# Placing the shared expert's output products and the state sums on TensorE in a selective-scan and MoE kernel

## The chip, the cores and the metric

The kernel runs on one core of a Trainium2 chip. Its metric is the device time of one execution in microseconds (us). Three runs of the kernel before gave 1494.33, 1497.56 and 1495.76 us, median 1495.76.

## The reference

The program is two layers of "cross-attention replaced by a selective scan" and a feed-forward part, on x of shape (4, 512, 512) and a context of shape (4, 512, 256):

```python
x = x + tanh(g_xattn[0]) * scan_layer(ctx_1024, layernorm(x), L0...)   # z = layernorm(x)
x = x + tanh(g_ffn[0])   * moe(layernorm(x), L0...)
x = x + tanh(g_xattn[1]) * scan_layer(ctx_1024, layernorm(x), L1...)
x = x + tanh(g_ffn[1])   * lora_ffn(layernorm(x), L1...)

# scan_layer, for one of 4 batches; 512 channels, 16 states, 512 steps
x = in_proj_w @ hidden; u = silu(conv4(x) + conv_b)
dt_lo, Bm, Cm = split(x_proj_w @ u); delta = softplus(dt_proj_w @ dt_lo + dt_proj_b)
state_t = state_{t-1} * exp(delta_t * A) + delta_t * u_t * B_t        # every channel and state
y_t = sum_n state_t[n] * C_t[n] + D * u_t;   y = y * silu(z)

# moe, per token, 16 experts, the best 4 by grouped routing
y_e = (silu(x @ gate_e.T) * (x @ up_e.T)) @ down_e.T
out = sum_e w_e * y_e + shared expert (the same form, for all tokens)
```

Everything is float32.

## The kernel before

Work is cut by batch and layer into eight stages: stages 0 to 3 are the scans of layer 0, stage 4 is the first scan of layer 1 (`FIRST_B` is 5, `NB` is 4), stages 5 to 7 are the other scans of layer 1 and run beside the tiles of the routed experts; a tail follows. Each engine runs a program of its own, written out by hand; they meet only at semaphores. An engine executes its program in order, so an instruction that waits holds up all that is written behind it.

A stage's scan is 32 units, four turns `i` of eight units `c`. I write a unit as (stage, turn, unit), for instance (4, 1, 3), and leave the stage out where it is plain. One unit covers one state and half of the 512 channels (256 channels as two rows of 128 partitions by 512 steps). It passes through four engines:

- ScalarE computes the decay exp(delta * A) (`decay`, line 712).
- VectorE multiplies du by B into PSUM (`mul_b`, line 1704), then does the scan (line 1712) into one of four slots `W[c % 4]`.
- GpSimd multiplies the slot by C (`mul_c`, line 457). It waits until the `mul_b` of the next unit is done.
- TensorE adds the slot to banks 0 and 1 by two products with the identity (`sum_state`, line 1095) and frees the slot. The scan four units later waits for that.

Between these units stand the other parts. Those that the change touches belong to the shared expert of the batch two stages back (`g`) or one stage back (`f`):

- `shared_in(b, it)`, line 1144: 16 rows of the trace (8 products) into the two auxiliary banks `AUX`; ScalarE's tanh (line 755) and VectorE's `shared_hidden` (lines 1736 and 1738) make the hidden half from them.
- `shared_out(b, (0, 1))` and `shared_out(b, (2, 3))`, line 1152: four products each, for two of the four row tiles, into `AUX[0]` and `AUX[1]`. VectorE's `shared_add` (line 1744) adds each bank to x. The second pair waits for `shacc`, that is, until VectorE has read the first.
- VectorE calls `shared_add(g, (0, 1))` after unit (s, 0, 7) and `shared_add(g, (2, 3))` after unit (s, 1, 2). These places are the same in both kernels.

After turn 1 of stage 4 comes the turn to the experts. VectorE ranks the last batch's tokens (`route`, from line 1536 on), does `shared_hidden(f, 0)`, and works out the slots (`slots`, from line 1598 on, with `shared_hidden(f, 1)` behind it). TensorE meanwhile has `shared_in`, two counting products (lines 1285 and 1286) which wait for `ranked` and for the first hidden half, `x_proj`, the second `shared_in`, and `stay_warm(PRE[1], 56)`, 56 products of 128 by 128 whose result nobody reads (line 1046). Turn 2 of stage 4 then mixes the units with eight `index_round`s (line 1172), each of which waits for masks from ScalarE (`mark_rows`) and VectorE (`mark_chunks`). Mask n uses a ring of three buffers: from n = 3 on it waits for index round n - 3.

Of the kernel before, what the change touches and what calls it, by code (L numbers as in the profile page):

```python
# [26 lines left out]
NB, L, D = 4, 512, 512  # L27
DM, NS, DR, DC = 256, 16, 16, 4
ET, QT, KC = D // P, L // P, DM // P
# [40 lines left out]
def build(nc, t):  # L70
    with ExitStack() as ctx:
# [80 lines left out]
        PRE = [PS[:, 4], PS[:, 5]]  # L152
# [853 lines left out]
        def _(pe):  # L1006
# [36 lines left out]
            def stay_warm(bank, n):  # L1043

                for _ in range(n):
                    nc.tensor.matmul(bank[:, 0:P], ID[:, :], ON[:, :], start=True, stop=True)  # L1046
# [100 lines left out]
            def shared_out(b, qs):  # L1147
                pe.wait_ge(shh_ready, IT * (b + 1))
                for q in qs:
                    for it in range(IT):  # L1150
                        at = 2 * WGU + it * D
                        mm = nc.tensor.matmul(AUX[q % 2], HB[:, it, q * P:(q + 1) * P], MW[:, 0, at:at + D],  # L1152
                                              start=(it == 0), stop=(it == IT - 1))
                    mm.then_inc(shdown_done, 1)
# [54 lines left out]
            for s in range(FIRST_B):  # L1209
                f, p, g = s - 1, s + 1, s - 2  # L1210
                if f >= 0:
                    conv(p, 0)
                    conv(p, 1)
                if f >= 0:
                    pe.wait_ge(yg_done, f + 1)
                sum_skip(s, 0)
                for c in range(HPT):
                    sum_state(s, 0, c)
                    if f < 0 and c == 0:
                        conv(p, 0)  # L1220
                        conv(p, 1)
                    if c == 0 and f >= 0:
                        if g >= 0:

                            pe.wait_ge(shh_ready, IT * (g + 1))
                        y_transposes(f, Y[:, yslot(f)], (0, 1))
                    if c == 1 and f >= 0:
                        in_proj(p, 1)
                        y_transposes(f, Y[:, yslot(f)], (2, 3))
                    if c == 3 and g >= 0:  # L1230
                        pe.wait_ge(xacc, QT * (f + 1))
                        shared_out(g, (0, 1))
                    if c == (6 if s == NB else 7) and g >= 0:

                        pe.wait_ge(shacc, QT * g + 2)
                        shared_out(g, (2, 3))
                    if c == 3 and f < 0:
                        in_proj(p, 1)
                    if f >= 0 and c in (4, 5):
                        conv(p, c - 2)  # L1240
                    if f < 0 and c == 5:
                        conv(p, 2)
                        conv(p, 3)
                if s == NB:
                    break
                for i in range(1, TURNS - 1):
                    for c in range(HPT):
                        sum_state(s, i, c)
                        if i == 1 and c == 1:
                            x_proj(p)  # L1250
                        if i == 1 and c in (4, 7):
                            dt_proj(p, c // 7)
                for c in range(HPT):
                    sum_state(s, TURNS - 1, c)
                    if c == 0 and f >= 0:
                        if g >= 0:
                            pe.wait_ge(shacc, QT * (g + 1))
                        norm_transposes(f, XN, range(ET))
                    if c == 1 and f >= 0:
                        route(f)  # L1260
                    if c == 2 and f >= 0:
                        shared_in(f, 0)
                    if c == 4:
                        in_proj(p + 1, 0)
                    if c == 5 and f >= 0:
                        shared_in(f, 1)

            s, f, p = NB, NB - 1, NB + 1
            for c in range(HPT):
                sum_state(s, 1, c)  # L1270
                if c == 1:
                    pe.wait_ge(shacc, QT * f)
                    norm_transposes(f, XN, (0, 1))
                if c == 2:
                    norm_transposes(f, XN, (2, 3))
                if c == 3:
                    route(f)
                if c == 5:

                    shared_in(f, 0)  # L1280

            pe.wait_ge(ranked, NB)
            pe.wait_ge(shh_ready, IT * f + 1)
            sel = SEL[:, :, :].rearrange("p t e -> p (t e)")
# [2 lines left out]
            x_proj(p)  # L1287
            pe.wait_ge(counts_read, 1)
            shared_in(f, 1)
            pe.wait_ge(u_ready, ET * (p + 1))  # L1290
            stay_warm(PRE[1], 56)
            shared_out(f, (0, 1))
            for c in range(HPT):
                if c == 0:
                    pe.wait_ge(shacc, QT * f + 2)
                    shared_out(f, (2, 3))
                else:
                    index_round(c - 1)
                sum_state(s, 2, c)
                if c in (3, 5):  # L1300
                    dt_proj(p, c // 5)
            for c in range(HPT):
# [790 lines left out]
```

## Time and profile before

| | |
|---|---|
| median of three runs | 1495.76 us |
| the profiled execution's own time | 1494.33 us |
| its span in the profile | 1492.6 us |
| TensorE busy | 1281.0 us (86%) |
| VectorE busy | 1352.1 us (91%) |
| ScalarE busy | 970.8 us (65%) |
| GpSimd busy | 785.6 us (53%) |
| granted TensorE clock, mean | 0.949 of full speed |

Times in the rows count from the span's start. PE is TensorE, DVE is VectorE, ACT is ScalarE, POOL is GpSimd. A float32 product of TensorE stands in the trace as two records, so x8 in a timeline row is four products. The ends of pipelined products are modelled: how long one group took is read better from the start of the next group. In a timeline row the last bracket is how long the engine stood idle before it, and who ended that.

### The profile page before, as it was taken

What the parts mean: (1) busy time and instruction counts of PE and PEld (TensorE: products, weight loads), DVE (VectorE), ACT (ScalarE), POOL (GpSimd) and SP (SyncE); (2) the same over time, 40 slices, a digit from 0 to 9 for tenths busy, and PEclk for the clock granted to TensorE, in tenths of its full rate; (3) what the DMA queues carried; (4) which work ended last, traced back from release to release, by engine and by line L of the source; (5) the groups of instructions that cost most, each with busy time, mean ns of one, the idle gap of its engine ahead of it and who ended that gap; (6) DMA issues with size and microseconds to landing.
All of it is one profiled execution on the core that took longest, in us unless ns stands there. A gap on an engine that the chain in (4) does not pass through costs nothing.

```text
span 1492.6 us, 14767 instructions
## 1 busy us (share of the span) xinstructions
PE 1281.0 (86%) x4630; PEld 740.3 (50%) x4630; DVE 1352.1 (91%) x1319; ACT 970.8 (65%) x1528; POOL 785.6 (53%) x411
## 2 busy tenths in 40 slices
PE   7785796899689869999989998899988899927988
PEld 3331242443244324455556676666766666616555
DVE  4999999899999999998998989999899989888894
ACT  5866568475866665635956788777887767734442
POOL 0465566545545553450565555665565665566632
PEclk9898899799999998999999999999999999977999
DMA  8354445535554553460466788787787887855531
GB/s 259 100 149 126 127 143 141 155 85 154 139 143 101 143 130 111 107 169 22 109 186 228 240 271 282 236 263 244 257 275 234 282 277 272 274 178 152 168 97 57
DMA packets 99838, 264.32 MB, mean 177 GB/s; under 512 B 10832, under 2 KB 11344, under 8 KB 93616
## 3 DMA queue, kind: packets, MB, share of 16 engines
q1 hardware_dynamic: 87936, 225.36, 50.5%
q0 software_dynamic: 11440, 37.50, 7.7%
q8 instruction: 37, 0.61, 0.2%
q10 hardware_dynamic: 384, 0.52, 0.1%
q14 instruction: 41, 0.34, 0.1%
HBM read 233.73 MB, written 29.62 MB: 176 GB/s over the span
## 4 chain that ended last, share of the span: by engine, by line
PE 41%; DVE 26%; issue 7%; ACT 6%; DMA 5%; POOL 4%; DVEq 0%; SPq 0%; ACTq 0%; POOLq 0%
DVE state L1712 11%; PE banks L1185 11%; DVE banks L1704 8%; PE banks L1196 6%; PE banks L1095 6%; DMA expert_w<-in_moe_w 3%; PE banks L1144 2%; PE banks L1164 2%; PE banks L1355 2%; PE banks L1039 2%; PE banks L1152 2%; ACT decay L712 2%; ACT L712 1%; POOL state L457 1%; PE banks L1016 1%
## 5 line engine op out<-in xcount | busy, mean ns | idle before, releaser
L457 POOL TENSOR_TENSOR state<-state,bc_rows 128x1024 f32<-128x1024 f32 x254 | 599.2, 2360 | 605.9 <-DVE banks L1704 605.7
L1712 DVE TENSOR_TENSOR_SCAN state<-decay,banks 128x1024 f32<-128x1024 f32 x176 | 401.9, 2284 | 15.7 <-ACT decay L712 6.6
L1095 PE MATMUL banks<-state,ident 128*128 128x512 f32 x640 | 330.0, 650 | 94.0 <-POOL state L457 93.8
L1704 DVE TENSOR_TENSOR banks<-du,bc_rows 128x1024 f32<-128x1024 f32 x256 | 314.5, 1228 | 13.4 <-DVE state L1712 0.5
L1185 PE MATMUL banks<-z_gate,expert_w 128*128 128x256 f32 (+1 forms) x1504 | 284.5, 347 | 6.4 <-DMA expert_w<-in_moe_w 6.4
L1185 PEld LDWEIGHTS banks<-z_gate,expert_w 128*128 128x128 f32 x1504 | 249.3, 191 | 59.4 <-issue 21.4
L1095 PEld LDWEIGHTS banks<-state,ident 128*128 128x128 f32 x640 | 121.3, 202 | 269.6 <-POOL state L457 153.6
L712 ACT ACTIVATE decay<-delta,neg_a 128x511 f32<-128x511 f32 x352 | 226.4, 710 | 16.4 <-DVE state L1712 11.2
L1712 DVE TENSOR_TENSOR_SCAN state<-expert_w,banks 128x1024 f32<-128x1024 f32 x80 | 182.9, 2286 | 7.7 <-ACT expert_w L712 5.1
L1196 PE MATMUL banks<-expert_w,hidden 128*128 128x512 f32 x316 | 156.0, 609 | 2.3 <-ACT expert_out L776 1.2
L1723 DVE TENSOR_TENSOR y_scan<-y_scan,state 128x1024 f32<-128x1024 f32 x94 | 114.3, 1216 | 3.6 <-POOL state L457 2.0
L712 ACT ACTIVATE expert_w<-delta,neg_a 128x511 f32<-128x511 f32 x160 | 104.1, 711 | 8.5 <-DVE state L1712 7.7
L762 ACT ACTIVATE z_gate<-banks 128x512 f32<-128x512 f32 (+1 forms) x94 | 49.6, 529 | 74.8 <-PE banks L1164 74.1
L712 ACT ACT_TABLE_LOAD x65 | 83.4, 1283 | 1.6 <-ACT x_dbl L578 0.4
L1046 PE MATMUL banks<-ones,ident 128*128 128x128 f32 x386 | 49.9, 290 | 28.9 <-DVE neg_mean_rstd L1935 28.9
L769 ACT ACTIVATE hidden<-banks 128x256 f32<-128x256 f32 (+1 forms) x94 | 33.2, 353 | 61.1 <-PE banks L1185 60.5
L1196 PEld LDWEIGHTS banks<-expert_w,hidden 128*128 128x128 f32 x316 | 54.4, 197 | 34.5 <-issue 30.9
L1046 PEld LDWEIGHTS banks<-ones,ident 128*128 128x128 f32 x386 | 49.0, 205 | 38.2 <-issue 38.2
L1144 PE MATMUL banks<-y_scan,expert_w 128*128 128x512 f32 x128 | 60.9, 632 | 3.4 <-DVE hidden L1738 3.4
L1730 DVE TENSOR_TENSOR hidden<-hidden,banks 128x256 f32<-128x256 f32 (+1 forms) x94 | 35.1, 373 | 31.3 <-ACT hidden L769 30.5
L769 ACT ACT_TABLE_LOAD x47 | 60.3, 1283 | 0.8
L1016 PE MATMUL banks<-ctx_t,in_w 128*128 128x512 f32 x96 | 47.8, 646 | 9.6 <-DMA ctx_t<-in_ctxT 7.2
(318 smaller groups left out, 1679.9 us busy)
## 6 DMA issues: line engine op xcount, KB each, us to landing
bc_rows<-bc_d SPq DMA_DIRECT2D x208, 512.0 KB, 4.9
expert_w<-in_moe_w SPq DMA_DIRECT2D x48, 1536.0 KB, 9.1
ys_d<-expert_out SPq DMA_DIRECT2D x32, 512.0 KB, 5.6
ctx_t<-in_ctxT SPq DMA_DIRECT2D x8, 512.0 KB, 6.7
x_res<-in_x SPq DMA_DIRECT2D x4, 1024.0 KB, 10.7
xn_d<-y_scan SPq DMA_DIRECT2D x4, 1024.0 KB, 7.5
ys_d<-expert_out SPq DMA_DIRECT2D x15, 256.0 KB, 5.7
out_x<-x_res SPq DMA_DIRECT2D x3, 1024.0 KB, 5.9
```

The costliest lines, as they stand in the source:

```text
L457: nc.gpsimd.tensor_tensor(W[:, c % 4], W[:, c % 4], bcast2(BC[:, u, 1, :]), ALU.mult).then_inc(mulc_done, 1)
L712: ins = nc.scalar.activation(DAS[c % n][:, m, 1:], DEL[:, s % 2, et, 1:], ACT.Exp, scale=AN[:, lay(s), et, state:state + 1])
L769: nc.scalar.activation(HT[:, j % 2, it, 0:n], GU(j, it)[:, 0:n], ACT.Silu).then_inc(sil_ready, 1)
L1016: mm = nc.tensor.matmul(pre_bank(s, et), INW[:, k, et * P:(et + 1) * P], CTX[:, k, :], start=(k == 0), stop=(k == KC - 1))
L1046: nc.tensor.matmul(bank[:, 0:P], ID[:, :], ON[:, :], start=True, stop=True)
L1095: mm = nc.tensor.matmul(PS[:, m], ID[:, :], W[:, c % 4, m, :], start=False, stop=True, skip_group_check=True)
L1144: mm = nc.tensor.matmul(AUX[g], MW[:, 0, at:at + P], XNT[:, k, :], start=(k == 0), stop=(k == ET - 1))
L1185: mm = nc.tensor.matmul(GU(j, it)[:, g * TILE:g * TILE + n], MW[:, u % 2, at:at + P], XST[:, k, 0:n], start=(k == 0), stop=(k == ET - 1))
L1196: mm = nc.tensor.matmul(out_bank(j, r), HT[:, u % 2, it, r * P:(r + 1) * P], MW[:, u % 2, at:at + D], start=(it == 0), stop=(it == IT - 1))
L1704: nc.vector.tensor_tensor(drive(s), DU[:, s % 2, 2 * h:2 * h + 2, :], bcast2(BC[:, u, 0, :]), ALU.mult).then_inc(mulb_done, 1)
L1712: nc.vector.tensor_tensor_scan(flat(W[:, c % 4]), flat(DAS[c % da_slots(s, i)]), flat(drive(s)), 0.0, ALU.mult, ALU.add).then_inc(scan_don ...
L1723: nc.vector.tensor_tensor(y, y, W[:, k % 4], ALU.add).then_inc(w_free, 1)
```

## The change

Only TensorE's program changes. The products `shared_out(g, (2, 3))` of stages 2, 3 and 4 are issued later: by one state sum in stages 2 and 3, by two in stage 4. They now stand behind the first sum of turn 1 in all three. In stage 4, `shared_in(f, 0)` goes from between the sums of units 5 and 6 to behind that of unit 7; the 56 warming products and a wait for `u_ready` ahead of them are gone; and in turn 2 the state sum of a unit is issued ahead of, not behind, the `shared_out` or `index_round` of the same step.

```diff
-                    if c == (6 if s == NB else 7) and g >= 0:
-
-                        pe.wait_ge(shacc, QT * g + 2)
-                        shared_out(g, (2, 3))
...
                     for c in range(HPT):
                         sum_state(s, i, c)
+                        if i == 1 and c == 0 and g >= 0:
+                            pe.wait_ge(shacc, QT * g + 2)
+                            shared_out(g, (2, 3))
...
             s, f, p = NB, NB - 1, NB + 1
             for c in range(HPT):
                 sum_state(s, 1, c)
+                if c == 0:
+                    pe.wait_ge(shacc, QT * (f - 1) + 2)
+                    shared_out(f - 1, (2, 3))
...
-                if c == 5:
-
-                    shared_in(f, 0)
-
+
+            shared_in(f, 0)
             pe.wait_ge(ranked, NB)
...
             shared_in(f, 1)
-            pe.wait_ge(u_ready, ET * (p + 1))
-            stay_warm(PRE[1], 56)
             shared_out(f, (0, 1))
             for c in range(HPT):
+                sum_state(s, 2, c)
                 if c == 0:
                     pe.wait_ge(shacc, QT * f + 2)
                     shared_out(f, (2, 3))
                 else:
                     index_round(c - 1)
-                sum_state(s, 2, c)
```

Below, TensorE's instructions stand in a row, before (-) and after (+). One x is one product here. First the end of turn 0 and the start of turn 1 in stage 2; stage 3 reads the same. Line 1095 is the state sum, two products a unit; 1152 is `shared_out`, 1058 `x_proj`.

```order
 L1039 MATMUL banks<-delta,expert_w 128x511
-L1095 MATMUL banks<-state,ident 128x512 x4
-L1152 MATMUL banks<-expert_w,hidden 128x512 x4
-L1095 MATMUL banks<-state,ident 128x512 x4
+L1095 MATMUL banks<-state,ident 128x512 x6
+L1152 MATMUL banks<-expert_w,hidden 128x512 x4
+L1095 MATMUL banks<-state,ident 128x512 x2
 L1058 MATMUL banks<-du,xproj_w 48x512 x4
```

`shared_out(g, (2, 3))` moved one unit's sum back; `x_proj` keeps its place. In stage 4 the same products move two sums back:

```order
-L1095 MATMUL banks<-state,ident 128x512 x2
-L1152 MATMUL banks<-expert_w,hidden 128x512 x4
-L1095 MATMUL banks<-state,ident 128x512 x6
+L1095 MATMUL banks<-state,ident 128x512 x6
+L1152 MATMUL banks<-expert_w,hidden 128x512 x4
+L1095 MATMUL banks<-state,ident 128x512 x2
 L1114 MATMUL banks<-ident,y_scan 128x128 x8
```

Line 1114, the transposes of the normed rows, keeps its place. Last, from the end of turn 1 to the first steps of turn 2 in stage 4: 1131 is TensorE's part of the routing, 1144 `shared_in`, 1046 the warming products, 1088 the start of the second half's sum, 1172 an index round.

```order
 L1131 MATMUL banks<-router_w,y_scan 128x16 x16
-L1095 MATMUL banks<-state,ident 128x512 x4
-L1144 MATMUL banks<-y_scan,expert_w 128x512 x8
-L1095 MATMUL banks<-state,ident 128x512 x4
+L1095 MATMUL banks<-state,ident 128x512 x8
+L1144 MATMUL banks<-y_scan,expert_w 128x512 x8
...
-L1046 MATMUL banks<-ones,ident 128x128 x56
-L1152 MATMUL banks<-expert_w,hidden 128x512 x8
-L1088 MATMUL banks<-y_scan,ident 128x512 x2
+L1152 MATMUL banks<-expert_w,hidden 128x512 x4
```

The first `shared_in` moved behind two more sums, and the second `shared_in` is followed at once by `shared_out`. The instructions of the other engines keep their order.

## Rows read from the trace of the kernel before

**Rows 1.** The page: the chain that ended last, by engine.

```profile
PE 41%; DVE 26%; issue 7%; ACT 6%; DMA 5%; POOL 4%; DVEq 0%; SPq 0%; ACTq 0%; POOLq 0%
```

**Rows 2.** Windows: bounds, length, busy us of PE, PEld, DVE, ACT, POOL; clock, DMA.

```profile
359.00:404.00 45.00, 33.71 (x73) 11.81 (x72) 43.11 (x26) 35.86 (x68) 28.24 (x12) 1.00 0.53 133
```

**Rows 3.** Timeline of PE, stage 2, units (0,6) to (1,1): start, us, group.

```profile
350.70 3.60 PE L1095 MATMUL banks<-state,ident 128*128 128x512 f32 x8
354.13 3.60 PE L1152 MATMUL banks<-expert_w,hidden 128*128 128x512 f32 x8
357.57 3.60 PE L1095 MATMUL banks<-state,ident 128*128 128x512 f32 x8
```

**Rows 4.** Timeline of DVE, the two adds of `shared_add(0, (2, 3))`.

```profile
356.44 0.72 DVE L1744 SCALAR_TENSOR_TENSOR x_res<-banks,tanh_gates,x_res 128x512 f32<-128x512 f32 x1
357.77 0.75 DVE L1744 SCALAR_TENSOR_TENSOR x_res<-banks,tanh_gates,x_res 128x512 f32<-128x512 f32 x1 [0.61 <-PE banks L1152]
```

**Rows 5.** Line 1744: what its idle time ended on, us and times, whole run.

```profile
  PE banks L1152: 3.0, 4
```

**Rows 6.** Timeline of POOL, the product of unit (2, 1, 0).

```profile
349.54 2.35 POOL L457 TENSOR_TENSOR state<-state,bc_rows 128x1024 f32<-128x1024 f32 x1 [1.34 <-DVE banks L1704]
```

**Rows 7.** Timeline of PE, stage 4: `shared_out(2, (2, 3))` and the sums behind it.

```profile
643.69 3.60 PE L1152 MATMUL banks<-expert_w,hidden 128*128 128x512 f32 x8
647.12 5.31 PE L1095 MATMUL banks<-state,ident 128*128 128x512 f32 x12
```

**Rows 8.** Timeline of DVE, stage 4: the same batch's adds, and scan (4, 1, 4).

```profile
646.67 1.40 DVE L1744 SCALAR_TENSOR_TENSOR x_res<-banks,tanh_gates,x_res 128x512 f32<-128x512 f32 x2
655.30 2.29 DVE L1712 TENSOR_TENSOR_SCAN state<-decay,banks 128x1024 f32<-128x1024 f32 x1 [2.40 <-ACT decay L712]
```

**Rows 9.** Timeline of PE, stage 4, from sum (1, 4) to the counting products.

```profile
661.70 6.34 PE L1095 MATMUL banks<-state,ident 128*128 128x512 f32 x8
667.87 7.03 PE L1144 MATMUL banks<-y_scan,expert_w 128*128 128x512 f32 x16
...
679.55 0.67 PE L1285 MATMUL banks<-selected,upper 128*128 128x256 f32 x2 [1.22 <-DVE hidden L1738]
```

**Rows 10.** Timelines of POOL, ACT and DVE in that stretch.

```profile
666.47 4.65 POOL L457 TENSOR_TENSOR state<-state,bc_rows 128x1024 f32<-128x1024 f32 x2 [1.35 <-DVE banks L1704]
...
674.94 0.60 ACT L755 ACTIVATE hidden<-banks 128x512 f32<-128x512 f32 x1 [12.82 <-PE banks L1144]
...
678.01 0.68 DVE L1736 SCALAR_TENSOR_TENSOR hidden<-hidden,banks 128x512 f32<-128x512 f32 x1
```

**Rows 11.** Timeline of PE, stage 4: the warming products and `shared_out(3, (0, 1))`.

```profile
691.12 12.67 PE L1046 MATMUL banks<-ones,ident 128*128 128x128 f32 x112
703.63 3.60 PE L1152 MATMUL banks<-expert_w,hidden 128*128 128x512 f32 x8
```

**Rows 12.** Timeline of DVE: end of `shared_hidden(3, 1)`, adds of (0, 1).

```profile
699.90 0.69 DVE L1738 TENSOR_TENSOR hidden<-hidden,banks 128x512 f32<-128x512 f32 x1
...
705.55 0.75 DVE L1744 SCALAR_TENSOR_TENSOR x_res<-banks,tanh_gates,x_res 128x512 f32<-128x512 f32 x1 [0.79 <-PE banks L1152]
707.26 0.75 DVE L1744 SCALAR_TENSOR_TENSOR x_res<-banks,tanh_gates,x_res 128x512 f32<-128x512 f32 x1 [0.97 <-PE banks L1152]
```

**Rows 13.** Timeline of PE in stage 3: a `shared_in` behind an idle stretch.

```profile
593.09 9.89 PE L1144 MATMUL banks<-y_scan,expert_w 128*128 128x512 f32 x16 [3.36 <-DVE hidden L1738]
```

**Rows 14.** Windows around that `shared_in`; columns as before.

```profile
592.00:596.00 4.00, 2.92 (x4) 1.40 (x5) 3.93 (x4) 3.97 (x6) 1.77 (x1) 0.50 0.01 2
596.00:600.00 4.00, 4.00 (x7) 1.70 (x7) 3.96 (x4) 4.00 (x7) 0.58 (x1) 0.66 0.57 101
```

**Rows 15.** Turns 2 and 3: ACT's mask 3 and decay (3, 4), DVE's scan (3, 4).

```profile
717.86 2.43 ACT L730 ACTIVATE y_scan<-expert_w 128x128 f32<-128x128 f32 x8
...
752.02 2.54 ACT L712 ACTIVATE decay<-delta,neg_a 128x511 f32<-128x511 f32 x4
...
755.65 2.29 DVE L1712 TENSOR_TENSOR_SCAN state<-decay,banks 128x1024 f32<-128x1024 f32 x1
```

## The prediction

> **What bounds the kernel now.** I read the chain of waits first. TensorE holds 41% of it and VectorE 26% [rows 1]; no engine bounds the whole kernel, so a move on TensorE is judged by what waits at its place. The windows say who leads in the scan stages: in the 45 us behind turn 0 of stage 2 VectorE is busy 43.11 us and TensorE 33.71 [rows 2]. There a late TensorE costs nothing and a late VectorE costs all. At the start of a stage it is the reverse: TensorE runs without a gap from the sums (0, 6) on [rows 3], and VectorE waits for it. The idle time of the `shared_add` line shows where: four waits for `shared_out`, 3.0 us in all [rows 5]. One is 0.61 us at the last add of stage 2 [rows 4]; stage 3 repeats it; the other two, 0.79 and 0.97 us, stand in stage 4 behind the warming products [rows 12]. Last I followed stage 4 by timelines of each engine. The change therefore matters at the places where VectorE waits for line 1152 or 1144.
>
> **Stages 2 and 3: `shared_out` behind one more sum.** Eight records of 512 columns take 3.43 us (350.70 to 354.13), so one unit's sum, four records, takes 1.72. TensorE has no gap here, and the sum that is pulled ahead, (1, 0), is ready: its GpSimd product ends at 349.54 + 2.35 = 351.9, before TensorE reaches it at 355.8 [rows 3, 6]. So `shared_out` ends 1.72 us later, at 359.3 instead of 357.6. VectorE was already waiting for that end: its last add starts at 357.77. It now starts at about 359.45, 1.68 later. `x_proj` behind it starts when it did. What the change frees sooner are slots of the scan ring, and no scan of this stretch waited for a slot. VectorE's program goes on without a gap, so nothing gives the 1.68 back: **2 x 1.68 = +3.4 us**. Bounds: 0 if something later absorbs both, 3.4 if nothing.
>
> **Stage 4, first half.** `shared_out(2, (2, 3))` started at 643.69 and ended at 647.12; the three sums behind it fill 5.2 us (5.31 with the modelled end), so they were ready or nearly so [rows 7]. With two of them ahead it ends at 650.56. VectorE comes to its adds at 646.67 [rows 8], does the first when TensorE's half is done (648.9) and the second at 650.65, ending near 651.35 instead of 647.99. That is 3.3 us late. But two units later VectorE had waited 2.40 us for a decay (655.30) [rows 8], and ScalarE's decay waits for TensorE's transposes, whose place and time stay (652.3). So the wait takes up 2.3 of the 3.3: **+1.0 us**, bounds 0 and 3.3.
>
> **The turn to the experts.** `shared_in(3, 0)` started at 667.87 behind the sums of units 4 and 5 [rows 9]. ScalarE made the tanh of it at 674.94, and VectorE picked it up only at 678.01, after its routing [rows 10]: 2.5 us of slack. Now the sums of units 6 and 7 stand ahead. GpSimd ends the product of unit 7 at 666.47 + 4.65 = 671.1, with the delay above 672.1; the sum takes 1.72, `shared_in` 6.87 (twice 3.43), tanh and handover 0.8: 681.5. By the other path, TensorE reaches the sums up to 3 us later than before, since the transposes and its routing products follow state products which wait for the delayed VectorE; then two slow sums (6.2 us, as in rows 9), two fast ones 3.4 and the same tail give about 682.3. VectorE's routing ends at 678.01 + 1.0 = 679.0 and now waits 2.5 to 3.3 us. Behind that wait stand `slots` and everything after it, and the counting products wait for VectorE as before (679.55) [rows 9]. **+3.0 us**, bounds 2.0 and 10 (the latter if `shared_in` runs at the low clock throughout, 6.9 more).
>
> **The warming products.** They hold TensorE from 691.12 to 703.8, while the hidden half that `shared_out(3, (0, 1))` needs is there at 700.6 [rows 11, 12]. So `shared_out` could start 3.2 us earlier. VectorE, however, has unit (4, 2, 0) and a mask to do first, until 704.76, and waited for TensorE only 0.79 + 0.97 = 1.76 us. This is all that can be won. Against it: without them TensorE is idle about 9.5 us ahead of `shared_out` (from the end of `shared_in`, 691.1 by the old times, to 700.6). In stage 3, after 3.36 us idle, a `shared_in` took 9.89 us against 7.03 for the same products elsewhere [rows 9, 13], and the granted clock was 0.50, then 0.66 [rows 14], that is the low level (1.2 GHz) for about five and a half microseconds of work: 2.9 us lost. With the same loss `shared_out` takes 3.43 + 2.9 = 6.3 us and ends at 706.9 (old times) against 707.1. So the gain is **-0.2 us**; bounds -1.8 (clock stays up) and +0.4 (all four products slow, 6.87).
>
> The Trainium skill, "TensorE: Matmul & The Clock Gate", section "HAM oscillation — how this bites in real kernels", puts the loss at half the throttled time and counts a whole burst behind a long idle stretch as throttled. The row of stage 3 agrees for the loss (about 5.6 us at the low level, 2.9 lost) but shows the clock up again within the burst. By the page the term here would be +0.4, by the row -0.2. Its table "Why this matters for your kernels" speaks against taking warming work away ahead of a burst.
>
> **Turn 2.** The sum ahead of the index round makes each round later by up to a state product and a sum. VectorE has no idle time here but the two waits named. ScalarE is nearly full: mask 3 (old start 717.86) [rows 15] waits for index round 0, which now follows sum (2, 1) and ends near 724. Taking VectorE's shift of about 4 us at that point off, ScalarE loses a further 2.2 us. Decay (3, 4), the first of the pair at 752.02, ends 1.3 later, at 753.3, and its scan starts at 755.65 [rows 15]: 2.3 us of slack. VectorE's own masks 3 to 7 wait for index rounds with 0.6 us to spare by the same replay, once short by 0.2. **+0.3 us**, bounds 0 and 3.
>
> **The sum.** 3.4 + 1.0 + 3.0 - 0.2 + 0.3 = +7.5 us. After stage 4 the kernel follows what VectorE and GpSimd hand over at the end of stage 4, by waits on their work, so the shift passes to the end. The profiled execution took 1494.33 us (1492.6 of span and 1.7 around it): 1501.8. It was the lowest of the three, 1.4 us under their median; I put the forecast of a median 0.7 above: **1502.5 us**, +0.45%. What a measurement of this kernel tells from no change is about 0.2%, 3 us, so the line to slower is 1498.8.
>
> **Rivals.**
> *Clock stays up and the moves are hidden* (faster). Place: `shared_out(3, (0, 1))`. If `shared_in` just before keeps the clock high over the idle stretch, VectorE's 1.76 us go. It decides only if the four delays above come to nothing, for instance because TensorE's queue at the stage starts is shorter than the rows say. Against it: the 0.61 us wait is direct evidence that VectorE is tied to that very end. 1494.33 - 1.8 = 1492.5, with the median's offset 1493. Chance 6%.
> *The stage starts absorb.* If the 1.68 us are taken up in the following stage (VectorE waits for decays at the next stage's start too), or the turn to the experts loses only 2.0, the sum is +4 or less: 1495 to 1499. Against it: those decays wait for TensorE, which is itself set off by VectorE's last units. Chance 14%.
> *`shared_in(3, 0)` slow.* With the sums of units 4 to 7 spread out by their waits, the clock may be low throughout; the granted clock after the routing products was already low for two sums (6.34 us for what takes 3.43). +6.9: 1509. Chance 8%.
> *Turn 2 stays slow.* If TensorE never got back to the high clock there, a sum and an index round take 6.9 us a unit against VectorE's 4.3: 8 x 2.6 = +21: 1523. Against it: stage 3's clock recovered under a load that is no denser. Chance 4%.
> *The forecast*, each delay as worked out: 68%.
>
> The range: 1498 to 1508 holds the forecast with its bounds and parts of the second and third rival. Slower: 68 + 8 + 4 + 3 (of the second rival) = 83%. Same: 11%. Faster: 6%.
>
> **What the changed profile would show.** (1) Idle time of line 1744 ended by line 1152: stages 2 and 3 with about 1.3 us before the first add and 1.0 before the second, and in stage 4 two waits, 2.2 and 1.0; with 1.4 us at the third `shared_out` in all near 9 us instead of 3.0. (2) A wait of VectorE of 2.5 to 3.3 us for ScalarE's tanh (line 755) ahead of line 1736 in stage 4, where there is none now. (3) TensorE idle near 9.5 us ahead of the third `shared_out`, its clock near 0.5 there, the group about 6.3 us long. (4) An idle time of ScalarE of about 2 us before mask 3, ended by an index round. (5) The start of the first expert tile's products 7 to 8 us later, and the rest of the span as long as before. The prediction is wrong if (1) shows no longer waits, or if the later stages end up with another length by more than 2 us.

## The result, and the profile after

| | changed kernel | kernel before |
|---|---|---|
| median, us (6 runs each) | 1507.30 (1505.57 to 1513.75) | 1495.99 (1494.33 to 1497.56) |
| ratio, 95% interval | 1.0089 (1.0067 to 1.0110) | |
| profiled execution, us | 1501.42 | 1494.33 |
| its span, us | 1499.7 | 1492.6 |

The change makes the kernel slower by 11.3 us of median, 0.9%. The forecast was +7.5 us on the profiled execution and 1502.5 us for the median. The profiled execution came out at +7.1, but it was quicker than all other runs of the same kernel. Three further times of that kernel are on record (1505.49, 1511.18 and 1512.48 us); the mean of all nine is 1509.25, and it is this that the ratio reflects: 0.89%, or 13.3 us (10.0 to 16.5). The direction was right and 1507.3 lies in the forecast's range (1498 to 1508), but the forecast change of the median, +6.7 us, is 40% below the 11.3 of the medians and half of what the ratio says. Two further rounds of the changed kernel gave 1.0074 and 1.0069. Each ratio below is against the kernel before as timed beside that run; medians of different rounds are not compared.

The engines' shares (the page's first part; busy us, share of the span, instructions) hardly moved:

```profile
PE 1261.5 (84%) x4518; PEld 721.7 (48%) x4518; DVE 1353.0 (90%) x1319; ACT 971.4 (65%) x1528; POOL 784.2 (52%) x411
```

The changed file's VectorE lines stand two lower: `shared_add` is 1742 (it was 1744), `shared_hidden` 1734 and 1736, the masks 1694, the scan 1710. Here is the idle time of line 1742 over the whole run, against 3.0 us in 4 waits before [rows 5]:

```profile
  PE banks L1152: 10.7, 9
```

The waits of VectorE in stage 4, 640 to 762 us (us in total, times, longest); the same stretch before had 2.4 us for a decay and 1.8 for line 1152, 4.2 in all:

```profile
DVE x_res L1742 <- PE banks L1152: 6.3, 5, 2.3
DVE expert_out L1694 <- PE banks L1172: 2.6, 1, 2.6
DVE hidden L1734 <- ACT hidden L755: 2.6, 1, 2.6
```

That is 11.5 us, 7.3 more than before. The entry of line 755 and most of the first were forecast; the one of line 1694, and 1.5 us of the first, were not. Timeline of VectorE, in order of time (start, us, group, idle time before it and what ended it): first stage 2's two adds, which answer to [rows 4]; then stage 4's, which answer to [rows 8], and the scan (4, 1, 4), which waits for no decay now; then the tanh that VectorE had not waited for in [rows 10]; then the third and fourth pair of adds; last a mask of turn 2.

```profile
354.71 0.75 DVE L1742 SCALAR_TENSOR_TENSOR x_res<-banks,tanh_gates,x_res 128x512 f32<-128x512 f32 x1 [1.25 <-PE banks L1152]
356.42 0.75 DVE L1742 SCALAR_TENSOR_TENSOR x_res<-banks,tanh_gates,x_res 128x512 f32<-128x512 f32 x1 [0.96 <-PE banks L1152]
...
646.80 0.75 DVE L1742 SCALAR_TENSOR_TENSOR x_res<-banks,tanh_gates,x_res 128x512 f32<-128x512 f32 x1 [2.30 <-PE banks L1152]
648.51 0.75 DVE L1742 SCALAR_TENSOR_TENSOR x_res<-banks,tanh_gates,x_res 128x512 f32<-128x512 f32 x1 [0.97 <-PE banks L1152]
...
654.13 2.29 DVE L1710 TENSOR_TENSOR_SCAN state<-decay,banks 128x1024 f32<-128x1024 f32 x1
...
679.51 0.69 DVE L1734 SCALAR_TENSOR_TENSOR hidden<-hidden,banks 128x512 f32<-128x512 f32 x1 [2.61 <-ACT hidden L755]
...
708.46 0.75 DVE L1742 SCALAR_TENSOR_TENSOR x_res<-banks,tanh_gates,x_res 128x512 f32<-128x512 f32 x1 [1.53 <-PE banks L1152]
...
718.33 0.75 DVE L1742 SCALAR_TENSOR_TENSOR x_res<-banks,tanh_gates,x_res 128x512 f32<-128x512 f32 x1 [0.51 <-PE banks L1152]
720.04 0.75 DVE L1742 SCALAR_TENSOR_TENSOR x_res<-banks,tanh_gates,x_res 128x512 f32<-128x512 f32 x1 [0.97 <-PE banks L1152]
...
739.83 0.82 DVE L1694 TENSOR_TENSOR expert_out<-expert_w,small 128x632 f32<-128x632 f32 x1 [2.62 <-PE banks L1172]
```

The last three rows are new. The kernel before did the fourth pair of adds in one go at 716.55, and its masks of turn 2 without a wait. The timeline of TensorE says why. The first row answers to the `shared_in` of [rows 9], the second to `shared_out(3, (0, 1))` of [rows 11]; then follow the sum (2, 0) with `shared_out(3, (2, 3))` behind it, and the sum (2, 4) with an index round behind it.

```profile
671.82 7.03 PE L1144 MATMUL banks<-y_scan,expert_w 128*128 128x512 f32 x16
...
702.15 6.27 PE L1152 MATMUL banks<-expert_w,hidden 128*128 128x512 f32 x8 [9.35 <-DVE hidden L1736]
...
712.89 2.54 PE L1095 MATMUL banks<-state,ident 128*128 128x512 f32 x4 [2.75 <-POOL state L457]
715.22 4.79 PE L1152 MATMUL banks<-expert_w,hidden 128*128 128x512 f32 x8
719.84 1.88 PE L1095 MATMUL banks<-state,ident 128*128 128x512 f32 x4
...
734.38 3.53 PE L1095 MATMUL banks<-state,ident 128*128 128x512 f32 x4
737.70 2.09 PE L1172 MATMUL banks<-expert_out,y_scan 128*128 128x79 f32 x16
```

The sum (2, 0) at 712.89 had waited 2.75 us for GpSimd's product, and it and the `shared_out` behind it ran in part at the low level of TensorE's clock: from 712.89 to 719.84 they took 6.95 us, where one and a half groups of 3.43 are 5.15. VectorE's adds came late by 0.51 and 0.97. The sum at 734.38 took 3.53 us where a sum takes 1.9, again at the low level. The index round waited behind it and ended at 739.8, and VectorE's mask starts there. The windows of the three stretches (bounds, length, busy us of PE, PEld, DVE, ACT, POOL, granted clock, DMA) show the level, 0.50 being 1.2 GHz and 1.00 being 2.4; a value between is a mean over both levels:

```profile
700.00:704.00 4.00, 1.85 (x2) 0.84 (x3) 3.79 (x6) 3.33 (x10) 0.00 (x0) 0.50 0.00 0
704.00:708.00 4.00, 4.00 (x7) 1.69 (x6) 2.93 (x3) 3.04 (x7) 0.00 (x0) 0.58 0.01 2
...
712.00:716.00 4.00, 3.11 (x5) 1.35 (x6) 3.97 (x4) 3.29 (x10) 2.04 (x2) 0.77 0.29 93
716.00:720.00 4.00, 4.00 (x9) 1.78 (x8) 2.57 (x3) 3.12 (x6) 1.15 (x1) 0.80 0.36 118
...
728.00:732.00 4.00, 3.40 (x19) 2.29 (x19) 3.97 (x4) 3.97 (x12) 2.04 (x2) 1.00 0.42 132
732.00:736.00 4.00, 4.00 (x12) 1.68 (x12) 3.97 (x4) 4.00 (x11) 2.04 (x2) 0.83 0.37 119
736.00:740.00 4.00, 4.00 (x20) 2.83 (x19) 1.38 (x2) 3.97 (x7) 1.39 (x1) 0.74 0.35 117
```

### Where the 11 us are

VectorE leads in the scan stages, so the distance between two of its scan starts is the time of a stretch. In us, from the scan rows of each trace; (s, i, c) is stage, turn, unit. A to D are the stretches that the change touches: A is (2, 1, 0) to (2, 1, 4), the same as (3, 1, 0) to (3, 1, 4) to 0.01; B is (4, 1, 0) to (4, 1, 4); C is (4, 1, 4) to (4, 2, 0); D1 is (4, 2, 0) to (4, 2, 4); D2 is (4, 2, 4) to (4, 3, 0). M is (2, 1, 4) to (3, 1, 0). "All" is (2, 0, 0) to (5, 0, 0), "rest" what lies outside.

| kernel | A | M | B | C | D1 | D2 | all | rest |
|---|---|---|---|---|---|---|---|---|
| before | 17.64 | 123.59 | 18.21 | 46.46 | 21.68 | 17.26 | 472.23 | 1020.37 |
| before_again | 17.63 | 123.56 | 18.21 | 46.48 | 21.66 | 17.29 | 472.23 | 1025.87 |
| changed | 19.36 | 120.97 | 19.29 | 49.14 | 23.01 | 19.86 | 480.74 | 1018.96 |
| after_again | 19.34 | 123.57 | 19.28 | 50.83 | 22.39 | 19.82 | 484.34 | 1022.36 |
| after_third | 19.35 | 120.98 | 19.28 | 49.16 | 23.02 | 19.86 | 480.74 | 1022.16 |
| after_old_order | 19.35 | 121.00 | 19.28 | 49.16 | 21.34 | 17.27 | 476.54 | 1019.76 |
| after_with_warming | 19.36 | 124.34 | 19.28 | 50.78 | 23.29 | 18.17 | 484.30 | 1022.40 |
| move_2_3_only | 19.36 | 124.50 | 18.21 | 46.45 | 23.33 | 17.26 | 478.19 | 1024.81 |
| shared_out_4_only | 17.63 | 123.62 | 19.28 | 46.45 | 22.38 | 17.28 | 474.03 | 1023.57 |
| shared_in_only | 17.64 | 123.55 | 18.20 | 49.17 | 21.67 | 17.27 | 474.91 | 1025.79 |
| no_warming | 17.63 | 123.56 | 18.21 | 46.46 | 20.85 | 17.27 | 471.39 | 1023.61 |
| order_only | 17.64 | 125.06 | 18.21 | 46.47 | 23.31 | 19.82 | 477.89 | 1028.71 |
| earlier_42 | 16.93 | 124.12 | 16.50 | 46.52 | 20.16 | 17.27 | 468.19 | 1027.81 |
| earlier_56 | 16.93 | 125.20 | 16.49 | 46.48 | 21.88 | 17.26 | 470.93 | 1021.37 |

Changed against before: A +1.72, twice; B +1.08; C +2.68; D +1.33 and +2.60; together 11.1 us, close to the 11.3 of the medians and within the ratio's 10.0 to 16.5. The profiled pair showed 7.1 because M came out 2.6 shorter and the rest 1.4 shorter. M takes either 121.0 or 123.6 and more in kernels with the very same code there. The traces show why: the sum (2, 3, 2) of stage 2, which follows TensorE's routing products, ran at the low level in the kernel before (granted clock 0.57 from 428 to 432 us), and at full clock in the changed one (1.00 from 424 to 432):

```profile
428.49 3.42 PE L1095 MATMUL banks<-state,ident 128*128 128x512 f32 x4
...
425.98 1.96 PE L1095 MATMUL banks<-state,ident 128*128 128x512 f32 x4
```

From its start to the next group it took 3.26 us in the first and 1.80 in the second, and VectorE's waits behind it are 0.95, 0.82 and 2.08 us against 0, 0 and 1.14. `after_again`, the same program as the changed kernel, has it slow (3.35 us) and the longer M. The rest differs by up to 5.5 us between two executions of the kernel before (1020.37 and 1025.87).

### The profile page after: what moved, and what is told of

It reads as the page before. It is cut to its first block and busy times, and to the rows that moved or that the text cites. A ratio compares the mean times of both kernels' runs of the same rounds, so it can differ in the third digit from the quotient of the medians.

```text
span 1499.7 us, 14543 instructions
## 1 busy us (share of the span) xinstructions
PE 1261.5 (84%) x4518; PEld 721.7 (48%) x4518; DVE 1353.0 (90%) x1319; ACT 971.4 (65%) x1528; POOL 784.2 (52%) x411
## 5 line engine op out<-in xcount | busy, mean ns | idle before, releaser
L1095 PE MATMUL banks<-state,ident 128*128 128x512 f32 x640 | 323.7, 638 | 106.6 <-POOL state L457 106.6
L1095 PEld LDWEIGHTS banks<-state,ident 128*128 128x128 f32 x640 | 118.0, 197 | 282.0 <-POOL state L457 170.0
L1046 PE MATMUL banks<-ones,ident 128*128 128x128 f32 x274 | 36.1, 290 | 28.4 <-DVE neg_mean_rstd L1933 28.4
L1353 PE MATMUL banks<-expert_w,du 128*128 128x512 f32 x128 | 55.6, 592 | 0.0
## 6 DMA issues: line engine op xcount, KB each, us to landing
x_res<-in_x SPq DMA_DIRECT2D x4, 1024.0 KB, 10.7
```

The source lines that it names most:

```text
L1095: mm = nc.tensor.matmul(PS[:, m], ID[:, :], W[:, c % 4, m, :], start=False, stop=True, skip_group_check=True)
L1353: nc.tensor.matmul(PS[:, q], xnt[:, q, k * P:(k + 1) * P], BW[:, k, :], start=(k == 0), stop=(k == ET - 1))
```

## The experiments

The theory after the result: the delays worked out for stages 2 to 4 are real and add up, and turn 2's order costs several us more than forecast. The rivals: the warming products matter; the turn to the experts is the large term; the differences are the clock's doing whatever the order.

**The changed kernel again**, no edit, twice.

> The changed kernel once more, for a second trace and more times. My theory: the waits that the first trace shows (8.5 us in stages 2 to 4) are fixed, and what the median has above it comes from TensorE's granted clock in turn 2 of stage 4, which is low for longer in most executions. So this trace, if its time is near 1507, has the same waits at lines 1152 and 755 within 0.5 us, and 3 to 6 us more of VectorE waiting for index rounds between 700 and 760 us. Rival: the extra 4 to 5 us lie outside stage 4 (start or expert phase), and turn 2 reads as in the first trace.

> A third trace of the changed kernel. Theory: from unit (2, 0, 0) to (5, 0, 0) it takes 480.7 to 484.5 us again, against 472.2 before, with the step of 1.72 in stages 2 and 3 each; the rest of its time against the other traces lies in stretches which the change doesn't touch. Rival: the step in stages 2 and 3 varies too.

Measured: 1.0074 (1.0053 to 1.0094) and 1.0069 (1.0040 to 1.0098). The third trace came out as expected. The theory for the second did not: turn 2 was 0.7 us shorter, not 3 to 6 longer, and the excess stood elsewhere: it ran C at 50.83 where the changed kernel had 49.14. The cause is one row, the sum (1, 2) of stage 4; here it is in the two traces, first in the changed kernel's:

```profile
652.96 1.98 PE L1095 MATMUL banks<-state,ident 128*128 128x512 f32 x4 [1.89 <-POOL state L457]
```

and in that of the repetition, which had fallen at the low level:

```profile
658.11 3.58 PE L1095 MATMUL banks<-state,ident 128*128 128x512 f32 x4 [1.89 <-POOL state L457]
```

It delayed the transposes behind it, and VectorE then waited 1.72 us for a decay:

```profile
664.65 2.29 DVE L1710 TENSOR_TENSOR_SCAN state<-decay,banks 128x1024 f32<-128x1024 f32 x1 [1.72 <-ACT decay L712]
```

The same program does the same sum at either level: part of what the change costs is drawn anew in each execution.

**The kernel before again**, no edit.

> The kernel before once more, for a second trace. Theory: units (2, 0, 0) to (5, 0, 0) take 472.2 us within 1.5, the waits at line 1744 are 3.0 us again, and differences to the first trace lie outside. Rival: the first trace was a lucky one in this stretch and the second takes 3 us or more longer, which would explain the gap between the forecast and the median.

Measured: 0.9991 (0.9972 to 1.0010). A to D repeat to 0.03 us, the rest is 5.5 us longer. Landmarks within the stages are good to hundredths, spans are not.

**No warming products.** The kernel before without them:

```
             pe.wait_ge(u_ready, ET * (p + 1))
-            stay_warm(PRE[1], 56)
```

> The kernel before, with only the 56 warming products removed. My theory as revised: the shared_out group costs what it did (-0.2 us), but turn 2 now has low-clock stretches that differ from one execution to the next: median +2 to +5 us, and a spread of 5 us or more. The prediction's own step said -0.2 and nothing more. Rival (warming is useless): -1.8 us, spread as before.

Measured: 1.0007 (0.9993 to 1.0020), so the revised theory of +2 to +5 us missed, and turn 2's D2 is as before (17.27). TensorE stood idle and then did `shared_out(3, (0, 1))` slowly, as in the changed kernel:

```profile
701.66 5.66 PE L1152 MATMUL banks<-expert_w,hidden 128*128 128x512 f32 x8 [9.45 <-DVE hidden L1737]
```

VectorE's waits at this pair of adds went from 1.8 to 1.0 us, and D1 is 0.8 shorter. The loss of the clock and the earlier start cancel to within a microsecond.

**The changed kernel with the warming products put back.**

> The changed kernel with the 56 warming products put back. If the missing warming is what the forecast undersized, the median falls from 1507 to about 1503 (fixed waits of stages 2 to 4 remain, +7 to +8) and the spread shrinks to 3 us. If the sums ahead of the index rounds are the cause, the median stays near 1507 with its spread.

Measured: 1.0073 (1.0053 to 1.0093), no better than without. Here the sum (2, 4) was fast, and the wait of the mask shrank from 2.6 to 0.9 us (us in total, times, longest):

```profile
DVE expert_out L1696 <- PE banks L1172: 0.9, 1, 0.9
```

So of the 2.6 in D2, 1.7 is the slow sum and 0.9 is there at full clock. The sum (2, 0) again waited 2.75 us, and it and the `shared_out` behind it took 6.95 us, with the same waits of 0.50 and 0.97: the warming products ahead of turn 2 did not change that. C had the slow sum (1, 2) again, and that took back what D2 gave.

**The move of stages 2 and 3 alone**, on the kernel before:

```
-                    if c == (6 if s == NB else 7) and g >= 0:
+                    if s == NB and c == 6:
...
                         sum_state(s, i, c)
+                        if i == 1 and c == 0 and g >= 0:
+                            pe.wait_ge(shacc, QT * g + 2)
+                            shared_out(g, (2, 3))
```

> The kernel before, with shared_out(g, (2, 3)) moved behind the first sum of turn 1 in stages 2 and 3 only. Theory: 2 x 1.7 = +3.4 us, since VectorE waits for its end and leads afterwards. Rival (the following stage absorbs it): 0.

Measured: 1.0027 (1.0012 to 1.0043), 4.0 us by the ratio; A is 1.72 longer in both stages. D1 was 1.65 longer too, with code there as before. Its trace shows an execution's own slow stretch: the counting products and `x_proj`, with granted clocks of 0.70 and 0.87 around them, took 6.24 us where the kernel before took 4.60. The warming products behind them then held `shared_out(3, (0, 1))` back, and VectorE waited 3.4 us at its adds instead of 1.8.

**The move of `shared_out` in stage 4 alone:**

```
-                    if c == (6 if s == NB else 7) and g >= 0:
+                    if c == 7 and g >= 0 and s < NB:
...
                 sum_state(s, 1, c)
+                if c == 0:
+                    pe.wait_ge(shacc, QT * (f - 1) + 2)
+                    shared_out(f - 1, (2, 3))
```

> The kernel before with only shared_out(2, (2, 3)) moved behind the first sum of turn 1 in stage 4. The prediction's step: +1.0 us, the rest of a 3.3 us delay absorbed by the wait for a decay. Theory now: +1.0 where sum (1, 2) runs at the high clock, +2.7 where it runs at the low one, since the second pair of transposes follows it and ScalarE's decay (1, 5) follows those. Rival: 0, all absorbed.

Measured: 1.0017 (1.0006 to 1.0027). B is 1.07 longer and C as before. Its timeline of VectorE shows the waits of the changed kernel to 0.01 us:

```profile
649.30 0.75 DVE L1747 SCALAR_TENSOR_TENSOR x_res<-banks,tanh_gates,x_res 128x512 f32<-128x512 f32 x1 [2.29 <-PE banks L1152]
651.02 0.75 DVE L1747 SCALAR_TENSOR_TENSOR x_res<-banks,tanh_gates,x_res 128x512 f32<-128x512 f32 x1 [0.97 <-PE banks L1152]
```

3.26 of new waits, less the 2.40 for the decay that are gone [rows 8], is 0.86; the other 0.2 lie in unit steps that show no wait.

**The move of `shared_in` alone:**

```
-                if c == 5:
-                    shared_in(f, 0)
-
+            shared_in(f, 0)
             pe.wait_ge(ranked, NB)
```

> The kernel before with only shared_in(3, 0) behind the sums of units 6 and 7 in stage 4. Theory: the tanh of it comes 2.5 us after VectorE's routing ends: +2.5 us, with a wait of that length ahead of line 1736. Rival (slack hides it): 0. Rival (the sums run at the low clock): up to +10.

Measured: 1.0024 (1.0012 to 1.0035). C is 2.71 longer, and the wait for tanh is there with the same 2.6 us though nothing else was changed; `shared_in` ran at full clock:

```profile
673.81 7.03 PE L1144 MATMUL banks<-y_scan,expert_w 128*128 128x512 f32 x16
```

**The order of turn 2 alone:**

```
             for c in range(HPT):
+                sum_state(s, 2, c)
                 if c == 0:
...
                     index_round(c - 1)
-                sum_state(s, 2, c)
```

> The kernel before with only turn 2 of stage 4 changed: each state sum ahead of the shared_out or index round of its step. The prediction's step: +0.3 us. My theory now: VectorE waits for the second add of shared_out(3, (2, 3)) (about 1 us) and, whenever the clock dips during a sum, for an index round (0 to 2.6 us): +1.5 to +4 us between units (4, 2, 0) and (5, 0, 0). Rival: the 2.6 us wait comes from the missing warming or the late start of turn 2, and the order alone costs under 0.5.

Measured: 1.0008 (0.9997 to 1.0020), though its trace has D longer by 1.63 and 2.56. Its waits and the two slow sums (TensorE's timeline, starts at 710 and 732):

```profile
DVE x_res L1744 <- PE banks L1152: 3.2, 4, 1.0
DVE expert_out L1696 <- PE banks L1172: 2.6, 1, 2.6
```

```profile
710.60 3.13 PE L1095 MATMUL banks<-state,ident 128*128 128x512 f32 x4 [2.75 <-POOL state L457]
...
732.34 3.38 PE L1095 MATMUL banks<-state,ident 128*128 128x512 f32 x4
```

The trace was taken of its slowest execution of twelve (1508.29; median 1501.35, against 1498.91 for the kernel before beside it). The timing allows at most 3.0 us, the trace shows 4.2: the two do not agree. With the slow sum (2, 4) absent the loss is 2.5 us, as in `after_with_warming` (D1 and D2 together 41.46 against 38.94), and this the timing allows; whether most executions of this kernel lack that slow sum is not shown. The next run asks from the other side.

**The changed kernel with the old order of turn 2**, the reverse of that edit.

> The changed kernel with only turn 2 of stage 4 put back: shared_out and the index rounds ahead of the state sums, as before. Theory (VectorE waits for index rounds behind slow sums): the wait of 2.6 us before line 1694 and the waits of the second shared_add pair go, the stretch from unit (4, 2, 0) to (5, 0, 0) takes within 1 us of the 79.3 us before, and the median falls by 2 to 4 us against the changed kernel. Rival (the order alone did nothing measurable by itself, 1.0008): the median stays.

Measured: 1.0047 (1.0025 to 1.0070), against 1.0089, 1.0074 and 1.0069 with the new order. D is back at 21.34 and 17.27, 4.3 us less than in the changed kernel; 0.0077 - 0.0047, from the mean of those three, is 0.3%, or 4.5 us; by the four intervals it is known to about 4 us either way, so the timing just shows that there is a gain, and the traces how large it is. TensorE dipped here too, a little later:

```profile
743.25 3.17 PE L1095 MATMUL banks<-state,ident 128*128 128x512 f32 x4
746.26 1.91 PE L1172 MATMUL banks<-expert_out,y_scan 128*128 128x79 f32 x16
```

and line 1694 shows no wait; `no_warming` has such a sum too (3.70 us at 741.81), without a wait. These two sums settle nothing, for they stand behind VectorE's last mask of turn 2 (740.67 and 738.72): no mask was left that could wait. What the old order is worth is read from the margin. Mask 6 waits for index round 3, and these are the two in the kernel before, TensorE's and VectorE's:

```profile
729.77 2.01 PE L1172 MATMUL banks<-expert_out,y_scan 128*128 128x79 f32 x16
...
734.27 0.94 DVE L1696 TENSOR_TENSOR expert_out<-expert_w,small 128x632 f32<-128x632 f32 x1
```

The round is done by 731.6, where the next sum starts, 2.6 us ahead of the mask: more than the 1.6 that one slow sum loses. With the new order the same mask is 0.9 us short at full clock. That a slow sum just ahead of round 3 would cost nothing in the old order follows from this margin; no trace has one there.

**The opposite direction.** If later costs, earlier should give. On the kernel before: `shared_out(g, (2, 3))` one sum earlier in stages 2 and 3, stage 4's transposes and routing one sum earlier, and 42 or 56 warming products:

```
-                    if c == (6 if s == NB else 7) and g >= 0:
+                    if c == 6 and g >= 0:
...
-                if c == 1:
+                if c == 0:
                     pe.wait_ge(shacc, QT * f)
                     norm_transposes(f, XN, (0, 1))
-                if c == 2:
+                if c == 1:
                     norm_transposes(f, XN, (2, 3))
-                if c == 3:
+                if c == 2:
                     route(f)
...
-            stay_warm(PRE[1], 56)
+            stay_warm(PRE[1], 42)
```

> The other direction, on the kernel before: shared_out(g, (2, 3)) one sum earlier in stages 2 and 3 (behind unit 6), the norm transposes of stage 4 one unit earlier (behind the sum of (1, 0)), and 42 warming products instead of 56. Theory: the waits of 0.61 us go twice, up to 1.7 of the 2.40 us wait for a decay goes, and the 1.76 us behind the warming products go: -4.5 us, 0.3%. Rival: the waits are replaced by others of the same length (ScalarE's decays): 0 to -1.5.

> The kernel of earlier_42 with all 56 warming products. Theory: the gain in stages 2 to 4 falls from 4.1 to 2.6 us (the 1.76 us wait is back) and the median is 1.5 us above earlier_42. Rival: the fewer warming products let the clock fall somewhere later and cost what they save: equal medians.

Measured: 0.9977 (0.9958 to 0.9996) with 42, 0.9991 (0.9979 to 1.0003) with 56. A is 0.7 shorter twice, B 1.7; D1 is 1.5 shorter with 42 only: 4.6 us in these stretches, as expected, and 3.4 by the ratio. VectorE's waits in stage 4 fell from 4.2 us to 1.0 with 42:

```profile
DVE state L1712 <- ACT decay L712: 0.7, 1, 0.7
DVE x_res L1744 <- PE banks L1152: 0.3, 1, 0.3
```

The version with 42 is the fastest measured, by 0.2% with an interval that ends just short of no difference, and 0.0014 from 56 is within the two intervals. Its spread was wide (1490.65 to 1508.27).

## Why the prediction was off

**Stages 2 and 3, +3.4.** Right: 2 x 1.72 = 3.43 in every trace with the move, and 1.25 and 0.96 us of waits where about 1.3 and 1.0 were forecast. Nothing absorbed it.

**Stage 4, first half, +1.0.** Right: +1.07 or +1.08 in every trace with the move, waits of 2.30 and 0.97 (forecast 2.2 and 1.0), and the decay wait gone. That the wait for the decay soaks up most of a 3.3 us delay is what the arithmetic had said.

**The turn to the experts, +3.0.** Right in mechanism and nearly in size: +2.68, with a wait for tanh of 2.61 us (forecast 2.5 to 3.3). In two of the six traces with the move it was 4.3, by the slow sum (1, 2), which the forecast did not have and whose clock changes from one execution to the next.

**The warming products, -0.2.** Right (the 3.2 us by which `shared_out` could start earlier is 3.0 when read from the start of its group, and nothing hangs on it): the waits at that pair of adds went from 1.76 to 1.53 us, TensorE was idle 9.35 us, the granted clock behind it was 0.50 and 0.58, and the group took 6.27 us (forecast: 9.5 idle, clock near 0.5, 6.3). Alone the removal measured 1.0007 (0.9993 to 1.0020). The burst recovered within itself, as the row of stage 3 had said; the other reckoning that the prediction gave, +0.4 with all four products slow, would have needed 6.87.

**Turn 2, +0.3: this is the term that was mis-sized.** D1 and D2 together are 42.87, 42.21 and 42.88 us in the three traces of the changed kernel, and 38.61 in the one that differs by this edit alone: 4.3, 3.6 and 4.3 us. The timing of the same pair gave 4.5, with about 4 either way, and `order_only` 4.2 by its trace. Two things were missing.

The first is in D1. The step spoke of the index rounds and left out that the same edit puts `shared_out(3, (2, 3))` behind sum (2, 0), which waits for GpSimd's product. One row of before would have shown that wait (GpSimd's timeline of the kernel before):

```profile
709.30 2.35 POOL L457 TENSOR_TENSOR state<-state,bc_rows 128x1024 f32<-128x1024 f32 x1 [38.18 <-DVE banks L1704]
```

The sum can't start before 711.7. At full clock, with 1.7 us of its own and 1.7 for each half of `shared_out`, the halves would be ready at 715.1 and 716.8 by the old times. VectorE's two adds began at 716.55 and about 717.2, so by these times the late producer alone would have cost nothing; no run has the new order without the clock loss that follows. The 2.75 us for which TensorE now stands idle come with a clock loss: the sum and `shared_out` took 6.95 us instead of 5.15 in all five traces with the new order, with the warming products (`after_with_warming`, `order_only`) and without, and with 1.8 us more the second half is ready at 718.6. VectorE's fourth pair of adds waits 0.51 and 0.97, 1.5 us. The prediction priced the low clock behind an idle stretch at `shared_out(3, (0, 1))`, and not here, where its own edit makes one.

The second is in D2. The step counted each index round late by a product and a sum at full clock, and found the masks with 0.6 us to spare, once short by 0.2. With a fast sum the mask waited 0.9 us, so the replay was off by that much; and one sum at the low level adds 3.53 - 1.92 = 1.6 us, which makes the 2.6. In all turn 2 cost 2.5 us without that slow sum and 3.6 to 4.3 with it. The upper bound of 3 was too small for the same two reasons. The rival *turn 2 stays slow* had the right cause for a large part, a low clock in turn 2, but as a lasting state; what happened is one group behind an idle stretch and single sums.

The Trainium skill, "TensorE: Matmul & The Clock Gate", section "What's actually happening", says of the slow products at the start of a kernel that their number differs from run to run, and puts that loss at under 1% of a typical kernel. These traces show the same variation in the middle of a kernel: the same sum took 1.98 and 3.58 us. The low clock cost 1.5 us in D1 and 1.7 in each of D2 and C where it struck, up to 4.9 us or 0.3% of the span. For a change that is worth 0.5% this is not small.

**What was to be seen.** (1) Near 9 us of waits for line 1152: 10.7, of which 9.2 where they were forecast and 1.5 in turn 2. (2) and (3) as forecast. (4) ScalarE idle about 2 us before mask 3: it was 4.40, the first sign of turn 2's larger term. ScalarE's timeline, where [rows 15] had no idle time:

```profile
723.55 2.44 ACT L730 ACTIVATE y_scan<-expert_w 128x128 f32<-128x128 f32 x8 [4.40 <-issue]
```

(5) The first expert tile's products 7 to 8 us later: 5.45 (780.94 before, 786.39 after), but this trace was 3.1 us ahead at the scan (2, 0, 0), which is in front of anything the change touches, and 2.6 at M.

**Adding up.** 3.43 + 1.07 + 2.68 + 4.26 - 0.34 (D1 with the old order, 21.34 against 21.68, for the warming products) = 11.1 us; the three ratios say 13.3, 11.1 and 10.3. The five parts taken alone give 0.27 + 0.17 + 0.24 + 0.07 + 0.08 = 0.83%, with an interval of about 0.3 either way, and the measured 0.69 to 0.89% lie in it. This is a weak test. One by one the timings say 4.0, 2.5, 3.6, 1.0 and 1.2 us and the traces 3.4, 1.1, 2.7, -0.8 and 4.2; all but the last agree within the timing's interval, and the agreement of the sums is in part luck. In the traces the stretches do add.

So of the 3.6 us or so between the forecast's +7.5 and these 11.1, turn 2 is 4.0, and the other four terms together are 0.4 the other way. A further 0.7 of the gap to the median is that the forecast set its median only 0.7 above the profiled time, where the kernel before had 1.4.

**What stays open.** Order alone measured 0.08% and at most 0.2%, while taking it back from the changed kernel gave 0.3%; the intervals overlap, and whether the other moves make the slow sum in D2 more frequent was not settled. Nor does any trace show what makes the clock fall at one sum and not at another.

## What to carry to other kernels

A step moved back on an engine costs its consumer the delay minus the wait that stood just behind it; worked out row by row this was right to about 0.3 us for four terms of five. When an edit swaps two things in a loop, go through the first iteration by itself: here it held a different operation behind a late producer, and the idle stretch that this made on TensorE brought the low clock with it, which turned a wait of nothing into 1.5 us. And where the consumer's margin is smaller than what one burst loses when TensorE's clock drops (1.6 us for one sum here), put the operation that others wait for ahead of the one that nobody waits for, or count that loss as a term.

## What the runs showed of the hardware

- The clock falls in the midst of steady work, not only behind idle time: TensorE was busy all 4 us of the window at 732 (granted 0.83), and for 3.40 of the 4 before it at 1.00.
- Behind an idle stretch of 2.75 us the six products of sum (2, 0) and `shared_out` took 6.95 us in all five traces with the new order, against 5.15 at full clock; behind 0.84 us idle, `shared_out(3, (2, 3))` of the kernel before took 3.54 for its four products, which is full clock.
- Where it falls in steady work changes with the execution. The sum (1, 2) of stage 4 took 1.98 or 3.58 us in the same program; the first slow sum in the second half of turn 2 started at 734.38 and 740.86 us in two traces of the changed kernel, and there was none in the kernel before from 720 to 748, whose windows all granted 1.00.
- 56 products of 128 columns, put in to keep the clock up over 9.4 idle us, were worth nothing here: 1.0007 (0.9993 to 1.0020) without them. They can cost: in `move_2_3_only` slow products ahead of them made them start 1.6 us late, and VectorE waited that much longer; in `after_again`, without them, the same kind of delay only shortened TensorE's idle time, from 9.35 to 7.65 us.
- The rest of the kernel, outside the stages of the change, differs by 5.5 us between two executions of one program, while A to D repeat to 0.03 us in its two traces. In the changed kernel A, B and D2 repeat to 0.04, C and D1 differ by 1.7 and 0.6 in one trace of three, each by how long a group ran at the low level, which a timeline shows. For a change of 0.5% one profiled pair is not enough as a measure of the total; stretch by stretch it is, with a second trace where a stretch holds a slow group. Two such groups, both in front of or beside the changed code, moved M by 2.6 us and D1 by 1.65.
